# The last FFN GEMM of a graph attention layer, turned: columns on partitions, the scale in ScalarE's copy, TensorE turning the result back

## The chip, the cores and the metric

The kernel runs on one core of a Trainium2 chip. Its engines work on their own instruction streams and wait for each other by semaphores: TensorE (PE) for matmuls and transposes, VectorE (DVE), ScalarE (ACT), GpSimd (POOL), and SyncE (SP), which issues DMAs here. The metric is the device time of one execution in microseconds (us).

## What is computed

One graph attention layer and one quantized feed-forward layer, on 384 nodes of 1024 features, in float32, with a residual around each:

```
x = x + gnn(layernorm(x))
x = x + ffn(layernorm(x))

ffn:  xq   = fake_quant(x)
      gate = xq @ wq(w_gate).T;  up = xq @ wq(w_up).T        # 352 hidden columns
      h    = fake_quant(silu(gate) * up)
      out  = h @ wq(w_down).T                                # 384 x 1024
```

fake_quant rounds to integers between -128 and 127 times one scale for the whole tensor; wq does so with one scale for each row of the weight, so for each output column of the GEMM. The last line is the GEMM that this case is about: 384 x 352 by 352 x 1024.

## The kernel before

The weights of the attention layer are streamed as 56 chunks of 512 KB. SyncE loads a chunk into `stage`, ScalarE rounds it into the high half of `ring`, GpSimd or VectorE subtracts to get the low half, and TensorE multiplies in three passes (`passes`, L687). This conveyor, projections and attention for 16 heads fill the span up to about 314 us. The feed-forward weights are quantized on the way (`load_ffn`, `ffn_turn`, `ffn_take`) and lie as bf16 integers in `guT` and `wdT`, 1024 output columns of `wdT` as three tiles of the 352 hidden rows (128, 128, 96; `I_TILES`). Their scales stand in `fsc`: for the last GEMM `fsc[:, 1, :, 1]`, one number for each output column, 128 partitions by 8.

In the order of every engine's program the end goes so. After the output projection TensorE turns the normalised rows (`turn_y`), ScalarE scales them (L650), VectorE rounds them to `xqT` (`round_off`, L1268 and L1269), TensorE computes gate and up (`gate_up`, L937), ScalarE does Silu (L655), VectorE multiplies and takes maxima (L1281, L1283), TensorE spreads the maximum over the partitions (`spread_max`, L917), and VectorE makes the scale and its reciprocal (`greatest`, L1206, L1207; `gmx[:, 10]` is the scale of h). ScalarE scales `hid` (L660) and VectorE rounds it into `hq`, hidden columns on partitions, 384 nodes along the free side, three tiles. `keep_clock` puts matmuls of no use into TensorE's waits.

The last GEMM runs over three tiles of 128 nodes and two halves of 512 columns, six output tiles in six PSUM banks (`DOWN`). Nodes are on partitions: the stationary side is a block of `hq`, the moving side half of `wdT`, three matmuls (hidden tiles) for each output tile (L961). The column scale therefore lies along the free side, and has to be the same on all partitions: `ds_bc` holds it as 128x1024. It gets there by a way of its own, long before: TensorE transposes the scales (L785), VectorE copies them to `ds_row` (L1120), SyncE stores them to DRAM between chunks 37 and 38 (L324) and loads them broadcast into `stage[:, 0]` after the last chunk (L328).

For each output tile VectorE multiplies PSUM by the scale of h and by `ds_bc` into `V2` (L1300). The left halves are then added to X by GpSimd (L455), the right ones by VectorE (L1304, behind its two scalings), and SyncE stores each half as soon as it is there (L334), six stores of 256 KB, rows of 2 KB. The order of all this is the order in which the program is written; no planner is at work.

Of the kernel before, what the change touches and what calls it, by code (L numbers as in the profile page):

```python
# [15 lines left out]
F32 = mybir.dt.float32  # L16
# [4 lines left out]
ALU = mybir.AluOpType  # L21
# [4 lines left out]
P = 128  # L26
N = 384
# [28 lines left out]


def gnn_ffn(nc, x, weights, biases, bias_o, edge_cols, edge_rows, edge_w, clips,
            w_gate_up, w_down, down_scale_row, codes, out):
    with ExitStack() as ctx:  # L60
        def sb(name, shape, dt):
            return ctx.enter_context(nc.sbuf_tensor(name, shape, dt))

        def sem(name):
            return ctx.enter_context(nc.semaphore(name))
# [42 lines left out]
        smx = sb("smx", [P, 4, 2 * NT], F32)  # L108
        wsc = sb("wsc", [P, 2, 4], F32)
        kinds = sb("kinds", [P, 4], F32)  # L110
        ds_row = sb("ds_row", [KT, P], F32)
        gmx = sb("gmx", [P, 13], F32)
        nmean = sb("nmean", [P, NT], F32)
        PS = ctx.enter_context(nc.psum_tensor("PS", [P, 8, HC], F32))
# [6 lines left out]
        def turn_bank(p, h, m):  # L121
# [20 lines left out]
        units = [area.rearrange("p (k n) -> p k n", k=4)  # L142
                 for area in [V2[:, u // 2, u % 2 * HC:(u % 2 + 1) * HC] for u in range(4)]
                 + [stage[:, 1, u * HC:(u + 1) * HC] for u in range(2)]]
        ds_bc = stage[:, 0, :]
        sig, hid = V2[:, :, 0:N], V2[:, :, HC:HC + N]
        blank = scratch[:, 3 * C:3 * C + N].rearrange("p (a n) -> p a n", a=1)

        gu_ps = PS[:, 2, :].bitcast(F16).rearrange("p (k i) -> p k i", k=KT)
# [1 line left out]

        WO, GATE, UP, DOWN, RED = ((0, 6), (7, 4), (5, 2)), (2, 5, 1), (0, 7, 3), (6, 2, 5, 1, 0, 7), (5, 4)
        TURNED = ((1, 0, 7), (3, 6, 4))

        def wo_chunk(c):
# [56 lines left out]
        o_high = sem("o_high")  # L214
        o_low = sem("o_low")
        soft_in = sem("soft_in")
        ds_turned = sem("ds_turned")
        ds_made = sem("ds_made")
        dsc_out = sem("dsc_out")
        dsbc_in = sem("dsbc_in")  # L220
        red_t = sem("red_t")
        red_b = sem("red_b")
        wo_full = sem("wo_full")
# [11 lines left out]
        ht_ready = sem("ht_ready")  # L235
        hq_ready = sem("hq_ready")
        d_full = sem("d_full")
        d_scaled = sem("d_scaled")
        y_out = [sem(f"y_out{i}") for i in range(2)]
        out_done = sem("out_done")  # L240

        class Chain:
# [19 lines left out]
        @block.sync  # L262
        def _(sp):
            def load(c, slot):
                sp.dma_start(stage[:, slot, :], weights[bass.ds(c, 1), :, :].rearrange("c p n -> p (c n)")
                             ).then_inc(stage_in[slot], 16)

            def load_ffn(s, turned):

                if turned:  # L270
                    sp.wait_ge(ffn_full, turned)
                i, j = s // 4, s % 4
                buf = FFN_BUF[s]
                if j < IT:
                    sp.dma_start(gu_in[buf], w_gate_up[IT * i + j:IT * i + j + 1, :, :].rearrange(
                        "s p (b n) -> p (s b) n", b=2)).then_inc(ffn_in[buf], 16)
                sp.dma_start(dn_in[buf], w_down[s:s + 1, :, :].rearrange("s p n -> p (s n)")
                             ).then_inc(ffn_in[buf], 16)

            for t in range(NT):  # L280
                sp.dma_start(X[:, t, :], x[t * P:(t + 1) * P, :]).then_inc(x_in[t], 16)
            for c in range(STAGE):
                load(c, c)

            def chunks(first, last):
                with sp.Fori(first // 2, last // 2) as i:
                    for j in range(2):
                        sp.wait_ge(w_low, 2 * i + (j - 1))
                        load(2 * i + j, j)

            def next_chunk(c):
                sp.wait_ge(w_low, c - 1)
                load(c, c % STAGE)

            next_chunk(2)
            sp.wait_ge(t_full, KT)
            load_ffn(0, 0)
            next_chunk(3)
            load_ffn(1, 0)
            next_chunk(4)  # L300
            load_ffn(2, 0)
            next_chunk(5)
            sp.wait_ge(blank_ready, 1)
            for b in range(LISTS):
                sp.dma_start(codes[b].rearrange("(m p n) -> p m n", m=NT, p=P), blank.to_broadcast([P, NT, N])
                             ).then_inc(codes_blank[b], 16)
            for c in range(6, 10):
                next_chunk(c)
            load_ffn(3, 1)
            next_chunk(10)  # L310
            load_ffn(4, 2)
            next_chunk(11)
            load_ffn(5, 3)
            next_chunk(12)
            next_chunk(13)
            load_ffn(6, 5)
            next_chunk(14)
            load_ffn(7, 6)
            for c in range(15, 18):
                next_chunk(c)  # L320
            chunks(18, 38)

            sp.wait_ge(ds_made, 1)
            sp.dma_start(down_scale_row.rearrange("(s p) -> s p", p=P), ds_row[:, :]).then_inc(dsc_out, 16)  # L324
            chunks(38, CHUNKS)
            sp.wait_ge(dsc_out, 16)
            sp.wait_ge(w_low, CHUNKS - 1)
            sp.dma_start(ds_bc, down_scale_row.rearrange("(a n) -> a n", a=1).to_broadcast([P, C])  # L328
                         ).then_inc(dsbc_in, 16)
            for m in range(NT):  # L330
                for hf in range(2):
                    cs = slice(hf * HC, (hf + 1) * HC)
                    sp.wait_ge(y_out[hf], m + 1)
                    sp.dma_start(out[m * P:(m + 1) * P, cs], X[:, m, cs]).then_inc(out_done, 16)  # L334
            sp.wait_ge(out_done, 16 * 2 * NT)


        @block.gpsimd
        def _(pool):
# [109 lines left out]
            pair_v(7)  # L449
            for c in range(53, CHUNKS):  # L450
                spare_low(c)

            for t in range(0, 2 * NT, 2):
                pool.wait_ge(d_scaled, t + 1)
                pool.tensor_tensor(X[:, t // 2, 0:HC], X[:, t // 2, 0:HC], V2[:, t // 2, 0:HC], ALU.add  # L455
                                   ).then_inc(y_out[0], 1)


        @block.scalar
        def _(act):  # L460
# [198 lines left out]
            for i, (_, iw) in enumerate(I_TILES):  # L659
                act.activation(hid[0:iw, i, :], hid[0:iw, i, :], ACT.Copy,  # L660
                               scale=gmx[0:iw, 12:13]).then_inc(ht_ready, 1)


        @block.tensor
        def _(pe):
# [4 lines left out]
            def keep_clock(n, columns=slice(0, N), bank=0):  # L670

                for _ in range(n):
                    pe.matmul(PS[:, bank, columns], wide[:, 0:P], wide[:, 0:columns.stop - columns.start],
                              start=True, stop=True)
# [105 lines left out]
            with pe.Fori(0, 2) as i:  # L780
                for j in range(4):
                    project(4 * i + (CK + j), 4 * i + (16 + j), j, XT)

            pe.wait_ge(ffn_evac, 8)
            pe.transpose(PS[0:KT, TPOSE, 0:P], fsc[:, 1, :, 1], ident[:, :]).then_inc(ds_turned, 1)  # L785

            def score(p, tiles):

# [163 lines left out]
                gate_up(1, 1, i)  # L952
            keep_clock(5, red_columns, RED[1])
            spread_max(1, 8, NT + 1)
            keep_clock(11, red_columns, DOWN[0])
            for t in range(2 * NT):
                m, hf = t // 2, t % 2
                for i, (_, iw) in enumerate(I_TILES):
                    if t == 0:
                        pe.wait_ge(hq_ready, i + 1)  # L960
                    ins = pe.matmul(PS[:, DOWN[t], :], hq[0:iw, i, m * P:(m + 1) * P],  # L961
                                    wdT[0:iw, i, hf * HC:(hf + 1) * HC], start=(i == 0), stop=(i == IT - 1))
                ins.then_inc(d_full, 1)


        @block.vector
        def _(dve):
# [147 lines left out]
            k_tile(7)  # L1115
            weight_of(1)
            weight_of(2)

            dve.wait_ge(ds_turned, 1)
            dve.tensor_copy(ds_row[:, :], PS[0:KT, TPOSE, 0:P]).then_inc(ds_made, 1)  # L1120

            def q_low(t):
                dve.wait_ge(proj_high, 2 * t + 25)
# [79 lines left out]
            def greatest(n):  # L1203

                dve.wait_ge(red_b, n + 1)
                chain.step(dve.tensor_reduce(gmx[:, 9 + n:10 + n], PS[:, RED[n], 0:P], X_AXIS, ALU.max))  # L1206
                return dve.reciprocal(gmx[:, 11 + n:12 + n], gmx[:, 9 + n:10 + n])  # L1207
# [69 lines left out]
            for i, (_, iw) in enumerate(I_TILES):  # L1277
# [6 lines left out]
                if i == 1:  # L1284
# [3 lines left out]
            dve.scalar_tensor_tensor(gmx[:, 8:9], gmx[:, 6:7], clip[:, 2, 1:2], gmx[:, 7:8], ALU.mult, ALU.max  # L1288
                                     ).then_inc(red_t, 1)
            greatest(1).then_inc(h_scale, 1)  # L1290
            for i, (_, iw) in enumerate(I_TILES):
                dve.wait_ge(ht_ready, i + 1)
                round_off(hid[0:iw, i, :], hq[0:iw, i, :]).then_inc(hq_ready, 1)

            dve.wait_ge(hq_ready, IT)
            dve.wait_ge(dsbc_in, 16)
            for t in range(2 * NT):
                m, cs = t // 2, slice(t % 2 * HC, (t % 2 + 1) * HC)
                dve.wait_ge(d_full, t + 1)
                dve.scalar_tensor_tensor(V2[:, m, cs], PS[:, DOWN[t], :], gmx[:, 10:11], ds_bc[:, cs],  # L1300
                                         ALU.mult, ALU.mult).then_inc(d_scaled, 1)
                if t % 2:
                    dve.wait_ge(d_scaled, t + 1)
                    dve.tensor_tensor(X[:, m, cs], X[:, m, cs], V2[:, m, cs], ALU.add).then_inc(y_out[1], 1)  # L1304


NAMES = ["x", "weights", "biases", "bias_o", "edge_cols", "edge_rows", "edge_w", "clips",
# [55 lines left out]
```

## Time and profile before

| | us |
|---|---|
| median of 3 runs | 349.96 |
| lowest and highest run | 349.65 to 352.48 |
| the profiled execution, its own time | 349.82 |
| its span, first to last instruction | 348.0 |
| TensorE busy | 324.3 (93%) |
| VectorE busy | 244.5 (70%) |
| GpSimd busy | 199.9 (57%) |
| ScalarE busy | 175.3 (50%) |

The profile comes from one execution. Busy shares are averages over the whole span; what an engine does to the end of the kernel is to be read from the chain of work that ended last and from the timeline of the last microseconds. Matmuls overlap, so the duration of one is longer than the distance between two.

### The profile page before, as it was taken

To read this page: it belongs to the slowest core of one execution; us is meant where nothing else is said; L and a number is where in the kernel's file an instruction comes from. 1 tells how busy PE (TensorE), PEld (TensorE's weight loads), DVE (VectorE), ACT (ScalarE), POOL (GpSimd) and SP (SyncE) were. 2 spreads that over 40 slices of the span, in tenths; PEclk is the share of its full clock that TensorE was granted. 3 is DMA by queue.
4 is the path that set the end of the run, shared out by engine and by line. 5 is a ranking of instruction groups with operands and counts; after the bars stand their busy time and mean duration, and the time that the engine had idled before them with its cause. 6 is when DMAs were issued, how large, how long until landed. Compare 5 with 4: busy or idle time off the path is not lost.

```text
span 348.0 us, 5814 instructions
## 1 busy us (share of the span) xinstructions
PE 324.3 (93%) x1990; PEld 292.4 (84%) x1990; DVE 244.5 (70%) x610; ACT 175.3 (50%) x327; POOL 199.9 (57%) x257
## 2 busy tenths in 40 slices
PE   5699999899999999999999899999999999998970
PEld 5599998687898999999899799999999788885630
DVE  4866699785046645279896878879788784778675
ACT  1443344557455333333374958668587685235210
POOL 6956557567777667589956573562745765000012
PEclk9999999999999999999999999999999999999997
DMA  7589336665224433833332330312303323000004
GB/s 262 181 313 333 128 119 202 205 208 168 92 79 156 130 121 121 285 108 114 121 124 67 115 116 6 122 31 93 113 10 121 94 90 121 2 0 0 2 12 169
DMA packets 16186, 42.23 MB, mean 121 GB/s; under 512 B 3496, under 2 KB 5920, under 8 KB 16160
## 3 DMA queue, kind: packets, MB, share of 16 engines
q1 hardware_dynamic: 13248, 39.40, 33.9%
q0 software_dynamic: 2064, 1.80, 1.8%
q10 hardware_dynamic: 848, 0.70, 0.6%
q8 instruction: 15, 0.25, 0.3%
q14 instruction: 11, 0.09, 0.1%
HBM read 38.51 MB, written 3.37 MB: 120 GB/s over the span
## 4 chain that ended last, share of the span: by engine, by line
PE 66%; DVE 10%; ACT 7%; DMA 6%; POOL 6%; issue 3%; SPq 1%; ACTq 0%; DVEq 0%
PE PS L690 50%; POOL ring L391 5%; DMA stage<-in_weights 5%; PE PS L816 4%; PE PS L792 4%; PE PS L804 4%; PE PS L937 2%; ACT ring L477 2%; DVE V L1300 1%; DMA X<-in_x 1%; DVE stats L974 1%; ACT scratch L569 1%; DVE X L1304 1%; ACT PT L487 1%; PE PS L736 1%
## 5 line engine op out<-in xcount | busy, mean ns | idle before, releaser
L391 POOL TENSOR_TENSOR ring<-stage,ring 128x256 fp32r<-128x256 f32 x128 | 101.0, 823 | 39.2 <-ACT ring L477 39.1
L690 PE MATMUL PS<-XT,ring 128*128 128x384 f32 x576 | 102.7, 336 | 1.6 <-DVE QT L1011 1.1
L690 PEld LDWEIGHTS PS<-XT,ring 128*128 128x128 f32 x576 | 99.6, 188 | 2.5 <-issue 2.4
L407 POOL DMA_INDIRECT codes<-ecol,place x51 | 59.7, 1170 | 25.8 <-issue 15.7
L477 ACT ACTIVATE ring<-stage 128x1024 fp32r<-128x1024 f32 x52 | 54.4, 1058 | 24.5 <-DMA stage<-in_weights 24.3
L1049 DVE TENSOR_TENSOR ring<-stage,ring 128x1024 fp32r<-128x1024 f32 x20 | 24.5, 1225 | 20.5 <-ACT ring L477 18.0
L690 PE MATMUL PS<-QT,ring 128*128 128x384 f32 x192 | 35.7, 340 | 0.5 <-POOL ring L391 0.5
L569 ACT ACTIVATE scratch<-scratch,smx 128x384 f32<-128x384 f32 x48 | 29.0, 608 | 12.6 <-DVE smx L1137 12.6
L690 PE MATMUL PS<-AT,ring 128*128 128x384 f32 x192 | 35.2, 338 | 0.0
L690 PE MATMUL PS<-ring,AT 128*128 128x512 f32 x144 | 34.6, 395 | 0.0
L690 PEld LDWEIGHTS PS<-AT,ring 128*128 128x128 f32 x192 | 33.1, 188 | 1.5 <-issue 1.5
L690 PEld LDWEIGHTS PS<-QT,ring 128*128 128x128 f32 x192 | 33.1, 188 | 1.1 <-POOL ring L391 0.8
L690 PEld LDWEIGHTS PS<-ring,AT 128*128 128x128 f32 x144 | 26.5, 188 | 5.3
L455 POOL TENSOR_TENSOR X<-X,V 128x512 f32<-128x512 f32 x3 | 3.8, 1265 | 45.8 <-DVE V L1300 45.8
L1137 DVE CUSTOM_DVE_ANT_0 scratch<-PS,scratch 128x384 f32<-128x384 f32 x48 | 24.3, 556 | 6.9 <-PE PS L792 6.8
L1003 DVE TENSOR_TENSOR PT<-PS,PT 128x384 fp32r<-128x384 f32 x48 | 23.1, 551 | 0.4 <-ACT PT L487 0.2
L1011 DVE SCALAR_TENSOR_TENSOR AT<-PS,bias,AT 128x384 fp32r<-128x384 f32 x16 | 9.9, 617 | 17.2 <-ACT AT L530 9.7
L487 ACT ACTIVATE PT<-PS 128x384 fp32r<-128x384 f32 x48 | 19.6, 502 | 1.0 <-PE PS L804 0.8
L1150 DVE TENSOR_SCALAR scratch<-scratch,smx 128x384 f32<-128x384 f32 x48 | 19.2, 457 | 0.6
L816 PE MATMUL PS<-PT,VA 128*128 128x384 f32 x96 | 19.4, 336 | 0.1
L804 PE MATMUL PS<-ident,scratch 128*128 128x128 f32 x144 | 17.7, 274 | 1.5 <-DVE scratch L1150 1.5
L804 PEld LDWEIGHTS PS<-ident,scratch 128*128 128x128 f32 x144 | 16.2, 140 | 2.7 <-DVE scratch L1150 2.3
(179 smaller groups left out, 467.6 us busy)
## 6 DMA issues: line engine op xcount, KB each, us to landing
stage<-in_weights SPq DMA_DIRECT2D x56, 512.0 KB
V<-in_w_gate_up SPq DMA_DIRECT2D x4, 512.0 KB, 3.8
codes<-scratch SPq DMA_DIRECT2D x3, 576.0 KB, 6.4
scratch<-codes POOLq DMA_DIRECT2D x3, 576.0 KB, 5.6
X<-in_x SPq DMA_DIRECT2D x3, 512.0 KB, 4.9
out<-X SPq DMA_DIRECT2D x6, 256.0 KB, 2.1
scratch<-in_w_gate_up SPq DMA_DIRECT2D x2, 512.0 KB
V<-in_w_down SPq DMA_DIRECT2D x5, 176.0 KB, 3.2
```

The source lines that it names most:

```text
L391: ins = pool.tensor_tensor(ring[1][:, slot, piece], stage[:, slot % STAGE, piece], ring[0][:, slot, piece].bitcast(F32), ALU.subtract)
L407: pool.indirect_dma_start(codes[b].rearrange("(n a) -> n a", a=1), bass.IndirectOffsetOnAxis(ap=place[:, t:t + 1], axis=0), ecol[:, VAL, t ...
L477: act.activation(ring[0][:, slot, :], stage[:, slot % STAGE, :], ACT.Copy).then_inc(w_high, 1)
L487: act.activation(dst, PS[:, bank, 0:N], ACT.Copy).then_inc(t_high, 1)
L569: ins = act.activation(SM[h][:, m, :], SM[h][:, m, :], ACT.Exp, scale=-1.0, bias=smx[:, 0, h * NT + m:h * NT + m + 1], accum_out=smx[:, 2, ...
L690: ins = pe.matmul(outs, lhs[a], rhs[b], start=start and n == 0, stop=stop and n == 2, skip_group_check=True)
L804: ins = pe.transpose(PS[:, turn_bank(u, h, m), n * P:(n + 1) * P], SM[h][:, n, m * P:(m + 1) * P], ident[:, :])
L816: ins = pe.matmul(PS[:, OUT, 0:N], VA[h][:, m, :], PT[h][s][:, m, :], start=(m, s) == (0, 0), stop=(m, s) == (NT - 1, 1))
L1003: dve.tensor_tensor(low, PS[:, bank, 0:N], high.bitcast(F32), ALU.subtract).then_inc(t_low, 1)
L1049: dve.tensor_tensor(ring[1][:, c % RING, :], stage[:, c % STAGE, :], ring[0][:, c % RING, :].bitcast(F32), ALU.subtract).then_inc(w_low, 1)
L1137: ins = dve.tensor_tensor_reduce(SM[h][:, m, :], PS[:, score_bank(p, h, m), 0:N], mask[:, m, :], -SCALE, 3e38, ALU.add, ALU.min, smx[:, 0, ...
L1150: ins = dve.tensor_scalar(SM[h][:, m, :], SM[h][:, m, :], smx[:, 3, h * NT + m:h * NT + m + 1], None, ALU.mult)
```

## The change

Six things change together, all of them for the last GEMM.

- The GEMM's sides are exchanged. The stationary side is a block of 128 columns of `wdT`, the moving side `hq` with all 384 nodes. There are 8 output tiles of 128 columns by 384 nodes, three matmuls each (`down`), in four PSUM banks used in turn.
- Columns now lie on partitions, so the scale is one number per partition: `dsc`, 128x8, made by one VectorE instruction behind `greatest(1)`. ScalarE copies each output tile from PSUM with this scale into `down_t` (areas of `V2` and `stage` that are free by then).
- TensorE turns each tile back with three float32 transposes into one of four other banks (`turn_back`). They are issued two tiles behind the matmuls.
- VectorE adds the turned tile to X, straight from PSUM, one instruction of 128x384 for 128 columns of all nodes. GpSimd has no part in it any more.
- SyncE stores X four times, each time 256 columns of all 384 nodes: 384 KB in runs of 1 KB.
- The way of the scales through DRAM (`ds_turned`, `ds_made`, `dsc_out`, `dsbc_in`, `ds_row`, `down_scale_row`) is taken out, and SyncE's two loops over chunks become one.

```diff
+        down_t = [sig[:, j, :] for j in range(NT)] + [stage[:, :, :].rearrange("p s c -> p (s c)")[:, j * N:(j + 1) * N]
+                                                      for j in range(KT - NT)]
-        WO, GATE, UP, DOWN, RED = ((0, 6), (7, 4), (5, 2)), (2, 5, 1), (0, 7, 3), (6, 2, 5, 1, 0, 7), (5, 4)
+        WO, GATE, UP, DOWN, RED = ((0, 6), (7, 4), (5, 2)), (2, 5, 1), (0, 7, 3), ((6, 2, 5, 1), (4, 0, 7, 3)), (5, 4)
...
-            chunks(18, 38)
-
-            sp.wait_ge(ds_made, 1)
-            sp.dma_start(down_scale_row.rearrange("(s p) -> s p", p=P), ds_row[:, :]).then_inc(dsc_out, 16)
-            chunks(38, CHUNKS)
-            sp.wait_ge(dsc_out, 16)
-            sp.wait_ge(w_low, CHUNKS - 1)
-            sp.dma_start(ds_bc, down_scale_row.rearrange("(a n) -> a n", a=1).to_broadcast([P, C])
-                         ).then_inc(dsbc_in, 16)
-            for m in range(NT):
-                for hf in range(2):
-                    cs = slice(hf * HC, (hf + 1) * HC)
-                    sp.wait_ge(y_out[hf], m + 1)
-                    sp.dma_start(out[m * P:(m + 1) * P, cs], X[:, m, cs]).then_inc(out_done, 16)
-            sp.wait_ge(out_done, 16 * 2 * NT)
+            chunks(18, CHUNKS)
+            for q in range(KT // 2):
+                cs = slice(2 * q * P, 2 * (q + 1) * P)
+                sp.wait_ge(y_out, 2 * q + 2)
+                sp.dma_start(out.rearrange("(m p) c -> p m c", p=P)[:, :, cs], X[:, :, cs]).then_inc(out_done, 16)
+            sp.wait_ge(out_done, 16 * (KT // 2))
...
-            for t in range(0, 2 * NT, 2):
-                pool.wait_ge(d_scaled, t + 1)
-                pool.tensor_tensor(X[:, t // 2, 0:HC], X[:, t // 2, 0:HC], V2[:, t // 2, 0:HC], ALU.add
-                                   ).then_inc(y_out[0], 1)
...
+            act.wait_ge(dsc_ready, 1)
+            for j in range(KT):
+                act.wait_ge(d_full, j + 1)
+                act.activation(down_t[j], PS[:, DOWN[0][j % 4], 0:N], ACT.Copy, scale=dsc[:, j:j + 1]).then_inc(d_scaled, 1)
...
-            pe.wait_ge(ffn_evac, 8)
-            pe.transpose(PS[0:KT, TPOSE, 0:P], fsc[:, 1, :, 1], ident[:, :]).then_inc(ds_turned, 1)
...
-            keep_clock(11, red_columns, DOWN[0])
-            for t in range(2 * NT):
-                m, hf = t // 2, t % 2
+            keep_clock(11, red_columns, DOWN[0][0])
+
+            def down(j):
+                if j >= 4:
+                    pe.wait_ge(d_scaled, j - 3)
                 for i, (_, iw) in enumerate(I_TILES):
-                    if t == 0:
+                    if j == 0:
                         pe.wait_ge(hq_ready, i + 1)
-                    ins = pe.matmul(PS[:, DOWN[t], :], hq[0:iw, i, m * P:(m + 1) * P],
-                                    wdT[0:iw, i, hf * HC:(hf + 1) * HC], start=(i == 0), stop=(i == IT - 1))
+                    ins = pe.matmul(PS[:, DOWN[0][j % 4], 0:N], wdT[0:iw, i, j * P:(j + 1) * P], hq[0:iw, i, :],
+                                    start=(i == 0), stop=(i == IT - 1))
                 ins.then_inc(d_full, 1)
+
+            def turn_back(j):
+                pe.wait_ge(d_scaled, j + 1)
+                if j >= 4:
+                    pe.wait_ge(y_out, j - 3)
+                for m in range(NT):
+                    ins = pe.transpose(PS[:, DOWN[1][j % 4], m * P:(m + 1) * P], down_t[j][:, m * P:(m + 1) * P], ident[:, :])
+                ins.then_inc(back_full, 1)
+
+            for j in range(KT):
+                down(j)
+                if j >= 2:
+                    turn_back(j - 2)
+            turn_back(KT - 2)
+            turn_back(KT - 1)
...
-            dve.wait_ge(ds_turned, 1)
-            dve.tensor_copy(ds_row[:, :], PS[0:KT, TPOSE, 0:P]).then_inc(ds_made, 1)
...
+            dve.tensor_scalar(dsc[:, :], fsc[:, 1, :, 1], gmx[:, 10:11], None, ALU.mult).then_inc(dsc_ready, 1)
...
-            dve.wait_ge(hq_ready, IT)
-            dve.wait_ge(dsbc_in, 16)
-            for t in range(2 * NT):
-                m, cs = t // 2, slice(t % 2 * HC, (t % 2 + 1) * HC)
-                dve.wait_ge(d_full, t + 1)
-                dve.scalar_tensor_tensor(V2[:, m, cs], PS[:, DOWN[t], :], gmx[:, 10:11], ds_bc[:, cs],
-                                         ALU.mult, ALU.mult).then_inc(d_scaled, 1)
-                if t % 2:
-                    dve.wait_ge(d_scaled, t + 1)
-                    dve.tensor_tensor(X[:, m, cs], X[:, m, cs], V2[:, m, cs], ALU.add).then_inc(y_out[1], 1)
+            for j in range(KT):
+                cs = slice(j * P, (j + 1) * P)
+                dve.wait_ge(back_full, j + 1)
+                dve.tensor_tensor(X[:, :, cs], PS[:, DOWN[1][j % 4], 0:N].rearrange("p (m n) -> p m n", m=NT), X[:, :, cs],
+                                  ALU.add).then_inc(y_out, 1)
```

## Rows read from the trace of the kernel before

**Rows 1.** The page: granted clock in 40 slices, and the closing chain by engine.
```profile
PEclk9999999999999999999999999999999999999997
...
PE 66%; DVE 10%; ACT 7%; DMA 6%; POOL 6%; issue 3%; SPq 1%; ACTq 0%; DVEq 0%
```

**Rows 2.** The closing chain in order of time (start, us, what), from 335.
```profile
335.13 0.37 DVE scratch L1269
...
335.55 0.40 PE PS L961
...
336.07 1.42 DVE V L1300 x2
...
342.62 1.20 DVE X L1304
```

**Rows 3.** The timeline of the end (start, us, instruction, [idle before, releaser]).
```profile
332.77 1.63 ACT L660 ACTIVATE V<-V,gmx 128x384 f32<-128x384 f32 x3 [2.65 <-DVE gmx L1207]
333.42 0.36 DVE L1268 TENSOR_SCALAR V<-V 128x384 f32<-128x384 f32 x1 [0.68 <-ACT V L660]
...
335.55 3.65 PE L961 MATMUL PS<-wdT,scratch 96*128 96x512 bf16 x16 [0.27 <-DVE scratch L1269]
...
342.01 1.26 POOL L455 TENSOR_TENSOR X<-X,V 128x512 f32<-128x512 f32 x1 [1.29 <-DVE V L1300]
```

**Rows 4.** The issues of L334 (stores) and L305 (pattern of three pieces).
```profile
L334 SPq DMA_DIRECT2D out<-X x6: 332/332/349, 338.2 to 343.9; - x6
...
DMA to landing us min/median/max: 2.0/2.1/2.2
...
L305 SPq DMA_DIRECT2D codes<-scratch x3: 435/490/1491, 27.1 to 28.2; - x3
```

**Rows 5.** Timeline around the 8x128 copy and the first scores: DVE, PE, PEld.
```profile
168.53 0.28 DVE L1120 COPY ds_row<-PS 8x128 f32<-8x128 f32 x1
...
169.84 3.40 PE L690 MATMUL PS<-QT,ring 128*128 128x384 f32 x18 [0.45 <-POOL ring L391]
173.16 1.84 PE L792 MATMUL PS<-K,Q 64*128 64x384 f32 x18
...
173.16 1.52 PEld L792 LDWEIGHTS PS<-K,Q 64*128 64x128 f32 x18 [0.25 <-DVE K L1129]
```

**Rows 6.** Timeline of the gate and up matmuls, second part.
```profile
324.78 5.36 PE L937 MATMUL PS<-scratch,guT 128*128 128x384 bf16 x32
```

**Rows 7.** Timeline of TensorE: four transposes, then fillers in bf16.
```profile
319.33 0.66 PE L911 MATMUL PS<-ident,V 128*128 128x128 f32 x4
319.82 1.95 PE L673 MATMUL PS<-wide 128*128 128x384 bf16 x11
```

**Rows 8.** Groups by form, 315 to 349 (busy us, mean ns | idle before).
```profile
L937 PE MATMUL PS<-scratch,guT 128*128 128x384 bf16 x32 | 5.7, 326 | 0.4 <-DVE scratch L1269 0.4
...
L655 ACT ACTIVATE V<-PS,wsc 128x384 f32<-128x384 f32 x2 | 1.2, 582 | 5.2 <-PE PS L937 5.2
...
L1263 DVE TENSOR_SCALAR wsc<-fsc,gmx 128x8 f32<-128x8 f32 x1 | 0.2, 227 | 0.0
```

**Rows 9.** L1003, additions out of PSUM: ns min/median/max, and four on the timeline.
```profile
L1003 DVE TENSOR_TENSOR PT<-PS,PT x48: 547/550/560, 182.0 to 287.8; 128x384 fp32r<-128x384 f32 x48
...
227.97 1.95 DVE L1003 TENSOR_TENSOR PT<-PS,PT 128x384 fp32r<-128x384 f32 x4
```

**Rows 10.** Windows: us, busy PE PEld DVE ACT POOL, granted clock, DMA share, GB/s.
```profile
194.00:199.00 5.00, 3.72 (x27) 3.17 (x26) 4.54 (x11) 4.90 (x15) 3.03 (x5) 1.00 0.30 105
...
339.00:339.50 0.50, 0.19 (x1) 0.00 (x0) 0.50 (x2) 0.00 (x0) 0.04 (x1) 1.00 0.90 340
...
344.00:344.50 0.50, 0.00 (x0) 0.00 (x0) 0.00 (x0) 0.00 (x0) 0.00 (x0) 0.61 0.75 283
...
345.00:345.50 0.50, 0.00 (x0) 0.00 (x0) 0.00 (x0) 0.00 (x0) 0.00 (x0) 0.50 0.97 369
```

**Rows 11.** DMA packets from 31.5 to 33.5, stores in rows of 1.5 KB.
```profile
DMA packets 546, 0.80 MB, mean 402 GB/s; under 512 B 22, under 2 KB 546, under 8 KB 546
```

More of the change, by code:

```diff
@@ L58, in gnn_ffn @@
 def gnn_ffn(nc, x, weights, biases, bias_o, edge_cols, edge_rows, edge_w, clips,
-            w_gate_up, w_down, down_scale_row, codes, out):
+            w_gate_up, w_down, codes, out):
     with ExitStack() as ctx:
@@ L110, in gnn_ffn @@
         kinds = sb("kinds", [P, 4], F32)
-        ds_row = sb("ds_row", [KT, P], F32)
+        dsc = sb("dsc", [P, KT], F32)
         gmx = sb("gmx", [P, 13], F32)
@@ L144, in gnn_ffn @@
                  + [stage[:, 1, u * HC:(u + 1) * HC] for u in range(2)]]
-        ds_bc = stage[:, 0, :]
         sig, hid = V2[:, :, 0:N], V2[:, :, HC:HC + N]
+        down_t = [sig[:, j, :] for j in range(NT)] + [stage[:, :, :].rearrange("p s c -> p (s c)")[:, j * N:(j + 1) * N]
+                                                      for j in range(KT - NT)]
         blank = scratch[:, 3 * C:3 * C + N].rearrange("p (a n) -> p a n", a=1)
@@ L216, in gnn_ffn @@
         soft_in = sem("soft_in")
[L217 to L220, printed above, removed]
         red_t = sem("red_t")
@@ L237, in gnn_ffn @@
         d_full = sem("d_full")
+        dsc_ready = sem("dsc_ready")
         d_scaled = sem("d_scaled")
-        y_out = [sem(f"y_out{i}") for i in range(2)]
+        back_full = sem("back_full")
+        y_out = sem("y_out")
         out_done = sem("out_done")
@@ L1356 @@
                            kind="ExternalInput").ap() for n in NAMES]
-    down_scale_row = nc.dram_tensor("down_scale_row", (C,), F32, kind="Internal").ap()
     out = nc.dram_tensor("out", (N, C), F32, kind="ExternalOutput").ap()
     codes = [nc.dram_tensor(f"codes{b}", (N * N,), F32, kind="Internal").ap() for b in range(LISTS)]
-    gnn_ffn(nc, *args, down_scale_row, codes, out)
+    gnn_ffn(nc, *args, codes, out)
     result = run_bass_kernel_spmd(nc, [arrays], core_ids=[0])
```

## The prediction

> **What bounds the kernel now.** I read the page first. TensorE makes 66% of the chain that ended last; its granted clock is full in every slice but the last [rows 1]. So the body is TensorE's, and a change to the last GEMM can only move the last few microseconds. Next comes the chain in order of time over the end [rows 2]. It says who owns them: the last rounded tile of `hq` is ready at 335.50, TensorE needs 0.40 us for the first output tile, and from 336.07 to 343.82 the chain is VectorE alone: three times two scalings of 128x512 (L1300) and one addition (L1304). The timeline shows the others over the same stretch [rows 3]: TensorE issues its 18 matmuls and is done at 339.20, GpSimd does three additions off the chain, ScalarE does nothing after 334.40. So the stage is 8.27 us long (335.55 to 343.82), 7.75 of them VectorE's, with 4.6 us of TensorE and all of ScalarE free. Then the last store: issued near 343.9, 2.1 us to landing [rows 4], and about 2 us of closing that any version has.
>
> **Removed.** The six scalings, six additions (three of each engine), six stores, and with them the whole path through DRAM of the weight scales: one transpose, one 8x128 copy (L1120), a 4 KB store and a 512 KB broadcast load. The load runs at 291, more than 40 us before its reader, so nothing ends later or earlier by it.
> The copy costs VectorE 0.28 us at 168.53; 4.3 us on, the first scores wait for VectorE's `K2`, and TensorE's weight loads stand idle 0.25 us before them [rows 5]. But the rows say that this idle lies between weight loads; the matmuls of L690 run up to 173.24 and those of L792 start at 173.16. I take 0 for it and keep 0.25 us of gain as the end of the range. The transpose (0.27 us long, overlapped) comes before a wait for a chunk from GpSimd of 0.45 us (169.84), which swallows it.
>
> **Added on TensorE.** For each of the 8 column blocks, 3 matmuls of bf16 with 384 columns and 3 float32 transposes of 128 columns. Matmuls of that shape: 32 in 5.36 us, 0.326 each from start to end, so (5.36 - 0.326)/31 = 0.162 us apart [rows 6]; one block takes 0.49. A transpose lasts 0.27, but that isn't what TensorE pays: four of them start at 319.33 and the bf16 matmul behind them at 319.82, so 0.12 each, with the change of type in it [rows 7]. Three take 0.36. A block is 0.85 us of TensorE.
> The Trainium skill ("TensorE: Matmul & The Clock Gate", Part 4: PE-mode transpose) has about 275 ns for a transpose inside a kernel. The duration in this trace agrees; as a distance it would make the sum 3.7 us longer, and that is a rival below.
>
> **Added on ScalarE.** 8 copies of 128x384 out of PSUM with a scale per partition. The nearest are L655, 0.58 us each, the same shape with a pointer scale [rows 8]. 0.58 is below TensorE's 0.85 a block, so ScalarE keeps up and shows only at both ends. The wait on `dsc_ready` holds nothing: the 128x8 product that it waits for is like L1263's (0.23 us) [rows 8] and falls into VectorE's idle 0.68 us before 333.42 [rows 3]. No table is loaded, since Copy already runs behind Silu at L660.
>
> **Added on VectorE.** 8 additions of 128x384, PSUM and SBUF. L1003 has that form: 0.55 each, four of them in 1.95, so 0.47 apart [rows 9]. Below 0.85 too, and one instruction per element instead of two. That X is read in three pieces of 128 is priced at nothing; nothing in the trace shows it, and the bound is L1304's 0.78 us for 384 of its 512 columns, an addition that shares its stretch with GpSimd's [rows 3]. GpSimd is out of the stage. At 0.78 VectorE still keeps up, and the end moves by 0.23.
>
> **The sum.** Start at 335.55, when the third `hq` tile is there (the first two matmuls of block 0 are done by then, as now). Block 0 is issued by 335.71. TensorE then runs down 1, down 2, back 0, down 3, back 1 and so on: down 7 is issued by 335.71 + 7 x 0.49 + 5 x 0.36 = 340.94. ScalarE's copy 0 ends at 335.55 + 0.33 + 0.12 + 0.58 = 336.58 (0.12 is the step from TensorE to VectorE, 335.95 to 336.07 [rows 2]), before back 0 is due at 336.69: no stall at the start. Down j+4 waits for copy j, which ended long before; back 4 waits for addition 0, 3 us old. At the end: down 7's last result is at 341.10, copy 7 runs 341.20 to 341.78, and back 5 and 6 (until 341.66) hide all but 0.1 us of it. Back 7 ends at 341.80 + 0.24 + 0.27 = 342.31, the last addition runs 342.40 to 342.95. Against 343.82 that is 0.87 us less.
> The last store doesn't pass all of it on. Now, two stores of 256 KB go out close together; their bytes flow from 344.0 to 345.5, at 369 GB/s in their last half microsecond [rows 10], and the last lands near 345.95. After, a store holds 384 KB in 384 runs of 1 KB instead of 128 of 2 KB. The nearest rows are runs of 1.5 KB, which came at 402 GB/s [rows 11]: 393 kB take 1.0 us. The pair before it (blocks 4 and 5) is added by 342.1 and its bytes flow from 342.95 to 343.95, 0.85 us after the issue as the first store does now (338.2, bytes from 339.05 [rows 4, 10]). The last is issued at 343.0, flows 343.95 to 344.95, and with the 0.45 us that lie now between last byte and landing it lands at 345.4; a slower issue (the one other pattern of three pieces takes 0.44 to 0.49 us against 0.33 [rows 4]) makes it 345.5. **Gain 0.45 us**: 0.87 from the engines, 0.42 given back by a larger last store. The profiled execution took 349.82, so 349.37; the median of the runs shown is 0.14 above it, so **349.5**.
>
> **Rivals.**
> (a) *More of it arrives.* The copy's 0.25 was on the path and the larger store costs nothing: 349.96 - 0.87 - 0.25 = 348.8. Against it is the idle that other engines cover in [rows 5]. 8%.
> (b) *Slower: the last store, bound by packets.* If a packet costs the same whatever it holds under 2 KB, the rows give 546 packets in 2 us over 16 engines, 59 ns each [rows 11]; 24 packets per engine are 1.41 us a store. The last two then flow 342.95 to 344.36 to 345.77, land at 346.2 instead of 345.95: 350.2. It decides once the two stores take over 1.28 us each. Against it: 1.5 KB at 402 GB/s is as fast by bytes as 2 KB, so bytes and not packets bound them so far. 14%.
> (c) *Transposes at their duration.* Three take 0.82, a block 1.31; down 7 is then issued by 343.24, back 5 to 7 end at 345.7, the last addition at 346.3, and its store costs 0.3 more than now: 349.96 + 2.5 + 0.3 = 352.8. The 0.49 us for four in [rows 7] speak against it. 4%.
> (d) *The clock.* The granted clock is 1.00 up to 344, through the stretch 194 to 199, where 18 transposes and waits lay among the matmuls, and it fell to its half (1.2 GHz) only in 344.0 to 344.5, 4.8 us after TensorE's last matmul [rows 10]. If a stage that is 40% transposes lost it from 337 on, the remaining 5 us of TensorE would take 10: about 354.5. The Trainium skill (the same section) says that the full clock doesn't engage for transposes; with the matmuls between them, this trace shows no loss. 3%.
> (e) *The body shifts.* Taking a copy out of VectorE's row could move the conveyor of chunks by some tenths either way, at the far end by more; no row gives it a sign. 3%.
>
> **How the numbers follow.** The forecast, a gain of 0.1 to 0.8 us, has 68%. A measurement of this kernel tells 1%, 3.5 us, from no change; of the cases (d) passes that, and (e) at its far end. The range goes down to (a) on the lowest run shown, 349.65 - 1.1 = 348.5, and up over (b), 350.2, with 0.7 for the runs' own spread (one of three was at 352.48, the other two 0.3 apart): 348.4 to 350.9. Faster by over 1%: 0.02, for a body that shifts. Slower by over 1%: 0.04. Within: 0.94.
>
> **What would show it.** In the changed profile: the chain over the end passes from VectorE to TensorE; matmuls in blocks of 0.49 us and three transposes in about 0.36, granted clock 1.00; ScalarE 8 times 0.58, VectorE 8 times 0.55 with idle before each; the last addition ending 7.4 us after the last `hq` instead of 8.3; and from that to the end of the span a stretch about 0.4 us longer than now (4.18 us). Transposes 0.27 apart, stores below 307 GB/s (393 kB in 1.28 us), or a VectorE that never idles would prove the steps wrong.

## The result, and the profile after

| | before | after |
|---|---|---|
| median of 20 runs each, us | 349.65 | 347.15 |
| ratio, 95% interval | | 0.9929 (0.9909 to 0.995) |
| the profiled execution, its own time | 349.82 | 347.09 |
| its span | 348.0 | 345.0 |

The kernel became 2.5 us faster (1.7 to 3.2 by the interval). Forecast were 0.45 us and 348.4 to 350.9: the time lies below the range. Two more sets of 12 runs of the same kernel, below, gave 0.9953 and 0.997; all three intervals lie below 1, the third only just (up to 0.9999), and the first says most. The chip has a slower state, and the ratios leave out the runs that fell into it: 4 of scale_way_back's 12, 2 of stores_single's 12, 1 of stores_mixed's 9, and of the kernel before's beside them 10 of 34 in one set and 2 of 17 in another.

Where it came from is read off two marks in the chain over the end: the end of the last rounded `hq` tile, and the end of the last addition. This is the chain of the changed kernel (start, us, what), to be laid beside [rows 2]; in it L949 are the matmuls of `down`, L958 the transposes of `turn_back`, L1299 the additions, and L650 in the timeline below ScalarE's copies.

```profile
334.12 0.37 DVE scratch L1269
334.48 0.05 issue
334.53 1.32 PE PS L949 x7
335.85 0.33 PE PS L958 x3
336.18 0.49 PE PS L949 x3
336.67 0.33 PE PS L958 x3
...
339.46 0.49 PE PS L949 x3
339.95 0.35 PE PS L958 x3
340.29 0.02 issue
340.32 1.02 DVE X L1299 x2
```

Between 334.53 and 340.3 the chain is TensorE's, 0.49 us of matmuls and 0.33 of transposes in turn. The timeline of the same stretch (start, us, instruction, [idle before, releaser]) has the last rounds of the others, to compare with [rows 3].

```profile
339.99 0.58 ACT L650 ACTIVATE stage<-PS,dsc 128x384 f32<-128x384 f32 x1 [0.24 <-PE PS L949]
340.32 1.49 DVE L1299 TENSOR_TENSOR X<-PS,X 128x384 f32<-128x384 f32 x3 [0.26 <-PE PS L958]
340.62 0.31 PEld L958 LDWEIGHTS PS<-ident,stage 128*128 128x128 f32 x3 [0.25 <-ACT stage L650]
```

The last addition ends at 341.81 (340.32 + 1.49): from the last `hq` tile 7.3 us instead of 8.3. So far it went as forecast. But the span ends 3.2 us after the last addition, where it had ended 4.2 us after it. The instructions of the frame around the kernel (they all stand on L60) say why. Before:

```profile
L60 POOLq DRAIN  x1: 5808/5808/5808, 342.0 to 342.0; - x1
...
L60 DVEq DRAIN  x1: 1236/1236/1236, 342.6 to 342.6; - x1
...
L60 SPq DRAIN  x1: 13/13/13, 346.2 to 346.2; - x1
L60 SPq EVENT_SEMAPHORE  x1: 17/17/17, 347.9 to 347.9; - x1
```

And after:

```profile
L60 POOLq DRAIN  x1: 6945/6945/6945, 290.3 to 290.3; - x1
...
L60 DVEq DRAIN  x1: 636/636/636, 341.2 to 341.2; - x1
L60 SPq DRAIN  x1: 13/13/13, 344.8 to 344.8; - x1
L60 SPq EVENT_SEMAPHORE  x1: 17/17/17, 344.9 to 344.9; - x1
```

The columns are ns min/median/max and first and last start. Each engine ends with a DRAIN, which in these rows begins while its engine's last work is still running and ends no earlier than that work, and then all meet at a barrier (the EVENT_SEMAPHORE rows). SyncE was through at 346.2 before, once the last store had landed. It then stood at the barrier until 347.9, for GpSimd's DRAIN, queued behind its last addition at 342.0, lasted 5.8 us and ended at 347.81. That addition ended at 343.27 ([rows 3], 342.01 + 1.26), so the drain took 4.5 us beyond it. In the changed kernel GpSimd's last instruction is a weight chunk at 290.36 of 2.40 us; the drain behind it ends at 297.2, again 4.5 us after, and nobody sees it.

```profile
290.36 2.40 POOL L415 TENSOR_TENSOR AT<-stage,AT 128x1024 fp32r<-128x1024 f32 x1 [0.30 <-ACT AT L468]
```

The page shows the emptied engine (GpSimd's busy tenths; before, these ended in 12).

```profile
POOL 6956657657677767589966572664726766000000
```

The stores, beside [rows 4], and the windows in which the last two moved their bytes (columns as in [rows 10]):

```profile
L324 SPq DMA_DIRECT2D out<-X x4: 372/380/400, 337.6 to 341.8; - x4
...
DMA to landing us min/median/max: 2.5/2.6/2.8
```

```profile
342.00:342.50 0.50, 0.00 (x0) 0.00 (x0) 0.00 (x0) 0.00 (x0) 0.00 (x0) 1.00 1.02 342
342.50:343.00 0.50, 0.00 (x0) 0.00 (x0) 0.00 (x0) 0.00 (x0) 0.00 (x0) 1.00 1.04 338
343.00:343.50 0.50, 0.00 (x0) 0.00 (x0) 0.00 (x0) 0.00 (x0) 0.00 (x0) 1.00 0.96 340
```

The DMA engines are full (share 0.96 to 1.04) at 340 GB/s. The granted clock is 1.00 through the stage and beyond it.

The difference of the two profiles from the last `hq` tile on is 12.5 - 10.5 = 2.0 us:

- the stage, 8.34 to 7.33: 1.0 us gained;
- last addition to SyncE's drain, 2.4 (346.2 - 343.82) to 3.0 (344.8 - 341.81): 0.6 lost to the larger last store;
- GpSimd's drain, which ended 1.6 us after SyncE's (347.81 - 346.2): gone.

The other 1.0 us of the 3.0 by which the spans differ lies ahead of the last `hq` tile (335.48 against 334.48), in code that is the same in both but for the way of the scales, and is treated below.

### The profile page after: what moved, and what is told of

The parts are those of the page before. It is cut to its first block, busy times and chain, and to the rows that moved or that the text cites. A ratio compares the mean times of both kernels' runs of the same rounds, so it can differ in the third digit from the quotient of the medians.

```text
span 345.0 us, 5874 instructions
## 1 busy us (share of the span) xinstructions
PE 325.6 (94%) x2019; PEld 294.7 (85%) x2019; DVE 241.3 (70%) x609; ACT 179.9 (52%) x335; POOL 195.2 (57%) x254
## 4 chain that ended last, share of the span: by engine, by line
PE 69%; DVE 8%; ACT 7%; DMA 6%; POOL 6%; issue 3%; SPq 1%; DVEq 0%; ACTq 0%
PE PS L679 52%; POOL ring L381 5%; DMA stage<-in_weights 5%; PE PS L802 4%; PE PS L778 4%; PE PS L790 4%; PE PS L923 2%; ACT ring L462 2%; DMA X<-in_x 1%; PE PS L949 1%; DVE stats L977 1%; ACT scratch L554 1%; ACT PT L472 1%; PE PS L725 1%; POOL QT L415 1%
## 5 line engine op out<-in xcount | busy, mean ns | idle before, releaser
L397 POOL DMA_INDIRECT codes<-ecol,place x51 | 58.8, 1152 | 25.8 <-issue 12.5
L554 ACT ACTIVATE scratch<-scratch,smx 128x384 f32<-128x384 f32 x48 | 28.9, 604 | 12.6 <-DVE smx L1137 12.6
L679 PE MATMUL PS<-ring,XT 128*128 128x512 f32 x72 | 17.6, 393 | 0.0
```

The lines of the kernel that those rows point to most:

```text
L397: pool.indirect_dma_start(codes[b].rearrange("(n a) -> n a", a=1), bass.IndirectOffsetOnAxis(ap=place[:, t:t + 1], axis=0), ecol[:, VAL, t ...
L554: ins = act.activation(SM[h][:, m, :], SM[h][:, m, :], ACT.Exp, scale=-1.0, bias=smx[:, 0, h * NT + m:h * NT + m + 1], accum_out=smx[:, 2, ...
L679: ins = pe.matmul(outs, lhs[a], rhs[b], start=start and n == 0, stop=stop and n == 2, skip_group_check=True)
```

## The experiments

Each row is one kernel, by its profile; the ratio is to the kernel before, run beside it. All times in us.

| kernel | last hq to last addition | from there to the end of the span | sum | ratio, interval |
|---|---|---|---|---|
| before | 8.3 | 4.2 | 12.5 | |
| after, first set | 7.3 | 3.2 | 10.5 | 0.9929 (0.9909 to 0.995) |
| after_again | 7.3 | 3.2 | 10.5 | 0.9953 (0.9925 to 0.998) |
| after_third | 7.3 | 3.2 | 10.5 | 0.997 (0.994 to 0.9999) |
| pool_late | 7.3 | 4.9 | 12.2 | 0.9999 (0.9968 to 1.003) |
| pool_mid | 7.3 | 3.2 | 10.5 | 0.9939 (0.9908 to 0.997) |
| before_no_pool | 9.0 | 2.4 | 11.4 | 1.0015 (0.9988 to 1.0043) |
| pool_two_of_three | 8.6 | 2.4 | 11.0 | 0.9966 (0.9929 to 1.0002) |
| scale_way_back | 7.3 | 3.2 | 10.5 | 0.9946 (0.9905 to 0.9987) |
| codes_first | 8.3 | 4.2 | 12.6 | 0.9994 (0.9969 to 1.002) |
| turn_back_one_behind | 8.2 | 3.0 | 11.2 | 0.9955 (0.9924 to 0.9987) |
| stores_single | 7.3 | 2.9 | 10.2 | 0.994 (0.9904 to 0.9975) |
| stores_single_again | 7.3 | 2.9 | 10.3 | 0.9939 (0.991 to 0.9967) |
| stores_mixed | 7.3 | 3.1 | 10.5 | 0.9922 (0.9882 to 0.9962) |

### The changed kernel again

> The changed kernel as it is, timed beside the kernel before on the same chip. Theory 1 (the gain is 1.0 us in the GEMM's stage and 1.7 us in the closing, where GpSimd's drain ended the kernel before, less about 0.7 us for larger last stores): 2 us below before, to within the 0.5 us by which the body shifts. Theory 2 (1 us of the gain is the body's, since the way of the scales through DRAM is gone): 3 us. Rival: the on-record forecast, 0.45 us below.

Measured: median 348.28 beside 349.74, 1.5 us, and its profile repeats the end to 0.02 us. The ratio, 0.9953, says 1.6 (0.0047 x 350).

> The changed kernel once more, as the neighbour of the two others and of the one with eight stores. 2.0 us below before, 10.5 us from the last hq tile to the end.

Measured: 349.0 beside 350.26, 1.3 us. By the ratios the gain is 2.5, 1.6 and 1.0 us in the three sets. Their mean is 1.7; the 2.0 us of the profiles lie inside the intervals of the first two sets and just inside that of the third (up to 2.1), and theory 2's 3 us is in the first alone, near its edge (3.2).

### GpSimd's drain: one instruction, late or not

```diff
             for c in range(53, CHUNKS):
                 spare_low(c)
+            pool.wait_ge(y_out, KT)            # pool_late; in pool_mid: pool.wait_ge(d_scaled, 4)
+            pool.memset(minus[:, :], 0.0)
```

> The changed kernel, with one instruction of GpSimd (a memset of 128x1 on a tile that is not used any more) behind the last addition. GpSimd's drain ended 4.5 us after its last instruction in both profiles. If that drain ends the kernel, it ends at 341.8 + 0.1 + 4.5 = 346.4 instead of the landing's 344.6, and the kernel is 1.6 to 1.8 us slower than the changed one. If the closing is set by the stores, no difference (under 0.2 us).

> The same instruction of GpSimd, but behind ScalarE's fourth copy, near 338.2 on the changed kernel's clock. Its drain would end at 342.8, before the last landing at 344.6. By the drain theory no difference from the changed kernel (under 0.2 us). If any late instruction of GpSimd costs (a contention, a wake-up), it is slower like the other one.

The memset lasts 0.1 us in both. pool_late, its timeline row and the two drains:

```profile
342.48 0.10 POOL L444 MEMSET minus<- 128x1 f32 x1 [49.30 <-DVE X L1302]
```

```profile
L60 POOLq DRAIN  x1: 4608/4608/4608, 342.5 to 342.5; - x1
L60 SPq DRAIN  x1: 13/13/13, 345.4 to 345.4; - x1
```

pool_mid:

```profile
L60 POOLq DRAIN  x1: 4607/4607/4607, 337.8 to 337.8; - x1
...
L60 SPq DRAIN  x1: 13/13/13, 345.3 to 345.3; - x1
```

The drain is the same 4.61 us in both. Where it starts at 342.5 it ends at 347.1, 1.7 us behind SyncE, and the end is 4.9 us after the last addition instead of 3.2; where it starts at 337.8 it ends at 342.4 and costs nothing. The runs point the same way: 349.41 against 347.39. Their 2.0 us are not the measure of the drain, though: after_again, run beside them and with the same end as pool_mid, stood at 348.28, so medians of these sets shift by some tenths without the end. The size, 1.7 us for the place of one memset, is the profiles'. The drain is shown.

### GpSimd out of the kernel before

```diff
-            for t in range(0, 2 * NT, 2):
-                pool.wait_ge(d_scaled, t + 1)
-                pool.tensor_tensor(X[:, t // 2, 0:HC], X[:, t // 2, 0:HC], V2[:, t // 2, 0:HC], ALU.add
-                                   ).then_inc(y_out[0], 1)
...
-                if t % 2:
-                    dve.wait_ge(d_scaled, t + 1)
-                    dve.tensor_tensor(X[:, m, cs], X[:, m, cs], V2[:, m, cs], ALU.add).then_inc(y_out[1], 1)
+                dve.wait_ge(d_scaled, t + 1)
+                dve.tensor_tensor(X[:, m, cs], X[:, m, cs], V2[:, m, cs], ALU.add).then_inc(y_out[t % 2], 1)
```

> The kernel before with GpSimd's three last additions moved to VectorE; scales, layout and stores stay. By the drain theory, with additions of 0.6 us once GpSimd no longer shares their stretch: VectorE needs 6 x 1.3 = 7.8 us as before, the last store lands near 346.0 and ends the kernel, 1.6 us faster than before. If the additions last 1.2 us by themselves, VectorE needs 11.6 us and the kernel is 2 us slower. If the closing has nothing to do with GpSimd, the same as before.

VectorE's last rows in it:

```profile
344.82 0.74 DVE L1295 SCALAR_TENSOR_TENSOR V<-PS,gmx,stage 128x512 f32<-128x512 f32 x1
345.60 0.69 DVE L1298 TENSOR_TENSOR X<-X,V 128x512 f32<-128x512 f32 x1
```

An addition is 0.69 us, not 1.20: beside GpSimd's it had been held up. The stage is 9.0 us (1.39 a pair, not the 1.3 expected), the closing 2.4: the end is 1.1 us shorter than before's. Yet the runs have no gain, where 1.6 us were expected (median 350.58 beside 349.74): the body of the profiled run was longer (last `hq` tile at 337.28), which is a matter of its own, below. By its times this run confirms nothing; its profile shows the shorter closing.

> The kernel before with the last of GpSimd's three additions given to VectorE (with a semaphore of its own for that store); the first two stay. By the drain theory GpSimd's last instruction ends near 340.7 on the profile's clock and its drain at 345.3, before the last landing. VectorE has one addition of 0.69 us more, but its last one no longer shares its stretch with GpSimd (0.69 instead of 1.20), so its last addition ends at about 344.0 instead of 343.8 and the last store lands at 346.4. From the last hq tile to the end 11.2 us instead of 12.5: 1.3 us faster than before, give or take the body. If the closing is no matter of GpSimd's last instruction: 0.2 us slower.

```diff
-            for t in range(0, 2 * NT, 2):
+            for t in range(0, 2 * NT - 2, 2):
...
-                if t % 2:
+                if t % 2 or m == NT - 1:
...
```

```profile
L60 POOLq DRAIN  x1: 5808/5808/5808, 341.0 to 341.0; - x1
...
L60 SPq DRAIN  x1: 13/13/13, 347.9 to 347.9; - x1
```

Measured: the same 5.8 us of drain, ended at 346.8, ahead of SyncE's. The end is 11.0 us (11.2 expected) and the kernel 1.2 us faster than before (0.0034 x 350; the interval just reaches no gain, 1.0002). One addition moved from one engine to another is worth 1.5 of the whole change's 2.0 us by the profiles, because the engine it is moved from is then done in time.

### The way of the scales, and the body

> The changed kernel with the way of the scales through DRAM put back as it was (transpose, 8x128 copy, 4 KB store between chunks 37 and 38, broadcast load after the last chunk, which ScalarE waits for and nobody reads). Theory A: the way itself costs nothing, or at most the copy's 0.25 us: within 0.3 us of the changed kernel (about 347.7). Theory B: the body's state hangs on it. Runs of before and of before_no_pool, which have it, show a granted clock that fell in the body in 18 of 47 runs, the changed kernel and its two variants in 8 of 56; then this one would fall in 4 or 5 of 12 and its median be 0.5 to 1 us above the changed kernel's.

Its end is that of the changed kernel, and its body lies within what the changed kernel's three profiles show (last `hq` tile at 335.57, between 334.48 and 335.98). The copy itself is settled by the changed kernel's trace, to be laid beside [rows 5]: without the copy, the weight loads stand idle the same 0.25 us before the first scores, and these start 3.34 us after the matmuls ahead of them (169.03 to 172.37), where it was 3.32 before. (In codes_first the copy ran nearer to the scores, at 169.68, and the idle was 0.35.)

```profile
172.37 1.52 PEld L778 LDWEIGHTS PS<-K,Q 64*128 64x128 f32 x18 [0.25 <-DVE K L1129]
```

The ratio, 0.9946, lies among the changed kernel's. Its runs were spread wider than others, so its interval would not tell 0.5 us. Theory B is not settled by it: the granted clock fell in 2 of the 8 runs that count.

> The kernel before with its DRAM tensor of scales declared behind the scatter's tables instead of ahead of them, so that the tables lie where the changed kernel has them; nothing else. If the place of the tables in DRAM sets how often the scatter ends late and the granted clock falls in the body, this kernel falls in 1 or 2 of 12 runs and is 0.5 to 1 us faster than before. Otherwise the same as before, within 0.4 us.

```diff
-    down_scale_row = nc.dram_tensor("down_scale_row", (C,), F32, kind="Internal").ap()
     out = nc.dram_tensor("out", (N, C), F32, kind="ExternalOutput").ap()
     codes = [nc.dram_tensor(f"codes{b}", (N * N,), F32, kind="Internal").ap() for b in range(LISTS)]
+    down_scale_row = nc.dram_tensor("down_scale_row", (C,), F32, kind="Internal").ap()
```

Measured: 0.9994, no difference from before that shows. The interval reaches from 1.1 us faster to 0.7 slower, so half a microsecond isn't excluded, but nothing points to the place of the tables in DRAM. Its profile repeats the end of the kernel before (8.3 and 4.2 us).

What the body does was found in the profile of before_no_pool. VectorE waits for the edge codes, which come back from the scatter by DMA, and behind that wait stand the roundings that TensorE needs:

```profile
150.96 1.36 DVE L1093 TENSOR_TENSOR scratch<-scratch 128x1152 f32<-128x1152 f32 x1 [7.35 <-DMA scratch<-codes]
...
153.02 3.24 PE L685 MATMUL PS<-XT,ring 128*128 128x384 f32 x9 [2.55 <-DVE AT L1006]
```

and the windows over it (busy PE, PEld, DVE, ACT, POOL, then granted clock, DMA share, GB/s):

```profile
152.00:154.00 2.00, 0.98 (x3) 0.98 (x4) 1.97 (x3) 1.06 (x1) 0.68 (x1) 0.77 0.78 262
154.00:156.00 2.00, 2.00 (x8) 2.00 (x7) 1.97 (x4) 0.00 (x0) 2.00 (x3) 0.50 0.00 0
156.00:158.00 2.00, 2.00 (x12) 2.00 (x12) 1.93 (x4) 0.00 (x0) 1.04 (x2) 0.88 0.00 0
```

TensorE stood 2.55 us, and its granted clock then was at its half (1.2 GHz) for about 3.5 us. In the profile of turn_back_one_behind it stood 2.34 us there, and the granted clock stayed at 1.00. In the profiles VectorE's wait for the codes was 3.8 to 4.8 us where TensorE didn't stand there at all (before, after, after_again, after_third, pool_mid, scale_way_back, stores_single, pool_two_of_three) and 5.5 to 7.4 us where it did, by 1.0 to 2.6 us (pool_late, stores_mixed, codes_first, stores_single_again, turn_back_one_behind, before_no_pool). It happened in kernels of both designs. In before_no_pool five of the 12 runs had a mean granted clock of 0.992 or more and 348.3 to 349.9 us, a sixth had 0.993 and 350.6; the other six had 0.989 or 0.99 and 350.6 to 352.3. Why one kernel meets it more often than another is open; its code up to there is the same in all of them.

### TensorE's order, and the stores

> The changed kernel with the turning back issued one tile behind the matmuls instead of two. ScalarE's copy takes 0.58 us and starts 0.1 us after the last result of a tile, which comes 0.16 us after its last matmul is issued; the next tile's matmuls cover 0.49 of these 0.85 us. TensorE would stand 0.35 us in each of 7 blocks: the stage 7.3 + 2.3 = 9.6 us and the kernel 2.3 us slower than the changed one. If TensorE's issue isn't what bounds the stage (VectorE or the stores do): under 1 us slower.

```diff
             for j in range(KT):
                 down(j)
-                if j >= 2:
-                    turn_back(j - 2)
-            turn_back(KT - 2)
+                if j >= 1:
+                    turn_back(j - 1)
             turn_back(KT - 1)
```

```profile
337.76 0.31 PEld L958 LDWEIGHTS PS<-ident,V 128*128 128x128 f32 x3 [0.63 <-ACT V L650]
...
341.17 0.31 PEld L958 LDWEIGHTS PS<-ident,stage 128*128 128x128 f32 x3 [0.24 <-ACT stage L650]
```

Measured: the stage 8.2 instead of 7.3 us. The direction is right, the size not: 0.9 and not 2.3 us. The expectation left something out: between the matmuls of a tile and its turning back lie not only the next tile's matmuls (0.49 us) but also the three transposes of the tile before (0.33). So 0.82 us are covered and not 0.49, and the blocks follow each other at 0.82 and 0.89 in turn. That makes about 0.2 us; about 0.4 come from the first tile, behind which only the next tile's matmuls lie (TensorE stands until 337.76), and 0.3 from the last, whose copy only one tile's transposes cover. The runs don't resolve it (0.9955, between the changed kernel's own sets).

> The changed kernel with eight stores of 128 columns (192 KB in runs of 512 bytes) instead of four. The changed kernel's runs of 1 KB moved at 340 GB/s, its last two stores back to back from 341.75 to 344.1. If bytes set the pace, a store takes 0.58 us, each is done before the next (0.82 us), only the last is left after the last addition, and the end comes 0.7 us earlier. If packets set it (48 ns a packet and engine as with 1 KB), a store takes 1.15 us, they pile up and the end comes 2.5 us later. In between, 35 ns: no change within 0.3 us.

> The changed kernel with eight stores, once more beside it on the same chip. Its first profile had 10.2 us from the last hq tile to the end, 0.3 us less than the changed kernel, and moved runs of 512 bytes at 290 GB/s. Expected 0.3 us below the changed kernel, if the difference is the stores' and not one profile's.

> The changed kernel with stores after additions 2, 4, 5, 6, 7 and 8: two of 384 KB early, four of 192 KB at the end. If bytes set the pace, 0.5 to 0.7 us earlier than the changed kernel. If packets of 512 bytes take 35 ns, the last four take 0.84 us each and follow the additions of 0.82, 0.5, 0.5 us: 0.2 us earlier. If 48 ns, 1.5 us later.

```diff
-            for q in range(KT // 2):
-                cs = slice(2 * q * P, 2 * (q + 1) * P)
-                sp.wait_ge(y_out, 2 * q + 2)
+            ends = (1, 2, 3, 4, 5, 6, 7, 8)     # stores_mixed: (2, 4, 5, 6, 7, 8)
+            for a, b in zip((0,) + ends, ends):
+                cs = slice(a * P, b * P)
+                sp.wait_ge(y_out, b)
...
```

Runs of 512 bytes, the windows of stores_single:

```profile
341.50:342.00 0.50, 0.00 (x0) 0.00 (x0) 0.00 (x0) 0.00 (x0) 0.00 (x0) 1.00 1.05 292
342.00:342.50 0.50, 0.00 (x0) 0.00 (x0) 0.00 (x0) 0.00 (x0) 0.00 (x0) 1.00 1.04 288
342.50:343.00 0.50, 0.00 (x0) 0.00 (x0) 0.00 (x0) 0.00 (x0) 0.00 (x0) 1.00 0.99 291
```

290 GB/s: a store of 197 kB takes 0.68 us, neither the 0.58 of bytes nor the 1.15 of packets. The last addition is followed by 2.9 us in both profiles, 0.3 less than with four stores. The two sets of runs stand at 0.994, the changed kernel's three at 0.9929 to 0.997, so this gain is shown by the profiles and not by the times. stores_mixed lies between them by its profile (3.1); its ratio, 0.9922, is the lowest of all, with an interval that holds every ratio of the changed kernel but the third. No version was clearly faster than the changed kernel; the one with eight stores is the shortest from the last `hq` tile to the end.

## Why the prediction was wrong

**What bounds the kernel** was read right up to the last addition and wrong behind it. The failed step is the first part's "about 2 us of closing that any version has". It was 2.0 us from the landing of the last store to the end of the span (345.95 to 348.0), and I took it for a fixed frame without asking what ends it. In the changed kernel 0.4 are left (344.6 to 345.0). 1.6 of the 2.0 were GpSimd's drain, a wait that hangs on when GpSimd gets its last instruction. The change takes GpSimd out of the stage (the prediction says so, and gives it no price), and with it the drain goes. pool_late and pool_mid show it with one memset. The sum thus lacked a term of 1.6 us, more than all the terms it had; with it the forecast would have been 347.9. Of the 2.35 us from the forecast 349.5 to the measured 347.15 the drain is 1.6, the start from a median of three runs 0.3 (349.96; of 20 runs it is 349.65), and about 0.5 stay open (the body, below).

**The removed way of the scales** cost nothing, as forecast; with it put back the end is the same, and the 0.25 us of idle that were kept as the low end of the range stand in the changed kernel too, without the copy. Rival (a) fails on both its terms: this one, and a larger store that costs nothing.

**TensorE's terms** held: 0.49 a block of matmuls, transposes at 0.11 each (0.33 for three, against 0.36 taken). Rival (c) is out.
**ScalarE** 0.58 and **VectorE** 0.56 each, both idle 0.24 and 0.26 us before each block; X read in three pieces cost nothing. The last addition came 7.33 us after the last `hq` tile, forecast 7.4. (The 3.7 us that the prediction puts on transposes at their duration count the last tile's, which the sum already had at 0.27; rival (c)'s own 3.3, from 349.5 to 352.8, is the figure that fits.)

**The last store** was mis-sized: 1 KB runs came at 340 GB/s, not at the 402 that runs of 1.5 KB showed [rows 11]. The time given back was 0.6 us and not 0.42. Rival (b) named the mechanism, but it isn't pure: runs of 2, 1.5, 1 and 0.5 KB moved at 381, 402, 340 and 290 GB/s (the 381 in the kernel before, from 344.50 to 345.00). Per packet and engine that is 86, 61, 48 and 28 ns (run length x 16 / rate), so neither bytes nor packets alone set it.

**The clock**, rival (d): the Trainium skill ("TensorE: Matmul & The Clock Gate", Part 4) has it that the full clock doesn't engage for transposes. The stage is 40% transposes and its granted clock was 1.00 throughout, up to 344.5. With matmuls of bf16 between the transposes the rule isn't seen.

**The body**, rival (e), was given 3% and some tenths. The identical kernel's last `hq` tile came at 334.48, 334.79 and 335.98 in three profiles. The first set's 2.5 us holds the 2.0 us of the end and about 0.5 that the other two sets don't confirm: they fall short of the 2.0 by 0.4 and 1.0. Whether the change moves the body at all is not shown, and that remainder is open.

The forecast's signs were right and its likeliest case, "a gain of 0.1 to 0.8 us", was not: the end alone gained 2.0.

## What to carry to other kernels

Ask of the last microseconds which engine ends them: look at every engine's DRAIN and at the barrier behind it, not only at the last store. An engine with a slow drain should get its last instruction early; here one addition less on GpSimd was worth 1.5 us by the profiles, and the whole change of layout, that addition included, 2.0. Before a fixed cost is written into a sum, name what would have to happen for it to be there.

## What the runs showed that I had not expected

- **GpSimd's drain.** 4.5 us from the end of its last instruction, whether that was a 128x1024 subtraction, a 128x512 addition or a 128x1 memset. The DRAIN of VectorE and of ScalarE ends within 0.1 us of their last instruction, and SyncE's lasts 13 ns. Why GpSimd's takes 4.5 us no run here shows.
- **Two engines on one port.** L1304 took 1.20 us beside GpSimd's addition and 0.69 without it. It starts at 342.62, GpSimd's ends at 343.27, and it ends 0.55 us after that [rows 2, 3]. The Trainium skill ("SBUF — State Buffer", Who interferes with whom) says that a VectorE instruction with two inputs in SBUF contends with a GpSimd instruction that reads SBUF, and that the ports they share are an exclusive lock. The trace agrees: 0.65 us of waiting and 0.55 of work. GpSimd's three additions thus took 3 x 0.69 us off VectorE and cost it 3 x 0.51: 0.5 us won for the stage by this reckoning, 0.7 by the two profiles (8.3 with them, 9.0 without), against 1.6 us of drain behind it.
